# Cross attention, experts and bit-linear layers in one program: where the experts' rows are put back, the order of the second queries, and the place of the output weights' products

## The reference

```python
x = x + L0_xattn(_layernorm(x), ctx)   # 16 heads of 16, plus a second attention on the last 16 context rows
x = x + L0_ffn(_layernorm(x))          # experts, below
x = x + L1_xattn(_layernorm(x), ctx)   # below
x = x + L1_ffn(_layernorm(x))          # bit-linear layers

def L0_ffn(x):                         # E = 16 experts, K = 2 of them for a token, CAP = 128 slots each
    xt = x.reshape(-1, D)                                  # 896 tokens, D = 256
    scores = jnp.sqrt(jax.nn.softplus(xt @ gate_w.T))
    _, idx = jax.lax.top_k(scores + gate_b, K)
    w = scores of the two, divided by their sum
    pos = ...                                              # place of the pair in its expert's slots
    valid = pos < CAP
    buf = zeros((E, CAP, D)).at[e, posc].add(x_pairs)      # rows without a place are dropped
    out = (jax.nn.silu(buf @ W1.T) * (buf @ W3.T)) @ W2.T  # 176 wide
    y_pairs = out[e, posc] * (w.reshape(-1) * valid)[:, None]
    return y_pairs.reshape(T, K, D).sum(axis=1) + (jax.nn.silu(xt @ Ws1.T) * (xt @ Ws3.T)) @ Ws2.T

def L1_xattn(x, ctx):                  # H = 16 heads of 128
    q = rmsnorm((x @ Wq).reshape(B, Sq, H, D), gq)
    k = rmsnorm((ctx @ Wk).reshape(B, Skv, H, D), gk)
    v = (ctx @ Wv).reshape(B, Skv, H, D)
    attn = softmax(einsum('bqhd,bkhd->bhqk', q, k) * D ** -0.5)
    return einsum('bhqk,bkhd->bqhd', attn, v).reshape(B, Sq, H * D) @ Wo
```

## Time and profile before

| what | value |
|---|---|
| median of 3 runs (lowest to highest) | 2377.38 us (2376.2 to 2377.73) |
| the profiled execution, and its span | 2380.05 us, 2378.2 us |
| mean granted TensorE clock in it | 0.935 |
| PE busy | 2121.2 us, 89% of the span |
| DVE busy | 1753.7 us, 74% |
| POOL busy | 1240.3 us, 52% |
| ACT busy | 1183.9 us, 50% |
| moved by the DMA engines | 243.79 MB, mean 103 GB/s |

### The profile page before, as it was taken

How to read it: one execution, slowest core, us unless ns; L and a number is a source line. 1 busy time by engine, 2 the same in 40 slices (tenths; PEclk the granted TensorE clock), 3 DMA queues, 4 the chain that set the end, 5 groups by cost and what they waited for, 6 DMA issues and landing times. The chain is left out here.

```text
span 2378.2 us, 46452 instructions
## 1 busy us (share of the span) xinstructions
PE 2121.2 (89%) x16728; PEld 1697.7 (71%) x16728; DVE 1753.7 (74%) x2341; ACT 1183.9 (50%) x2067; POOL 1240.3 (52%) x993
## 2 busy tenths in 40 slices
PE   4899999999999479999998792978999999999865
PEld 2688788788788357777777541656999999998633
DVE  5788887888888556666674434769999999998367
ACT  1688888888888225565554121542333333333202
POOL 1566666666665133344331113306999999997100
PEclk8999999999999669999999776989999999999977
DMA  2324324324322313334330432342222222220400
GB/s 86 90 93 157 121 92 157 121 94 155 121 106 119 138 67 130 114 121 146 129 112 30 184 93 71 112 135 95 84 80 85 84 102 75 88 93 22 182 0 16
DMA packets 97713, 243.79 MB, mean 103 GB/s; under 512 B 31313, under 2 KB 69106, under 8 KB 88290
## 3 DMA queue, kind: packets, MB, share of 16 engines
q1 hardware_dynamic: 91442, 228.87, 27.3%
q10 hardware_dynamic: 4608, 9.44, 1.0%
...
...
## 5 line engine op out<-in xcount | busy, mean ns | idle before, releaser
L347 DVE TENSOR_REDUCE rk<-n_sq 128x1024 f32 (+2 forms) x384 | 465.8, 1213 | 123.1 <-ACT n_sq L295 120.7
L295 ACT ACTIVATE n_sq<-n_slot 128x1024 f32<-128x1024 f32 (+1 forms) x384 | 394.7, 1028 | 142.7 <-PE n_slot L255 133.2
L253 PE MATMUL n_slot<-n_wh,n_yh 128*128 128x512 f32 (+1 forms) x768 | 318.1, 414 | 9.4 <-PEq L444 9.4
L1704 DVE TENSOR_REDUCE a_mpart<-a_pre 112x2 f32<-112x1024 f32 (+1 forms) x192 | 218.8, 1184 | 118.7 <-PE a_pre L1542 118.7
L255 PE MATMUL n_slot<-n_wh,n_yl 128*128 128x512 f32 (+1 forms) x768 | 302.9, 394 | 0.0
L254 PE MATMUL n_slot<-n_wl,n_yh 128*128 128x512 f32 (+1 forms) x768 | 302.3, 394 | 0.0
L1640 ACT ACTIVATE a_pr<-a_sc 128x448 f32<-128x448 f32 (+1 forms) x384 | 205.4, 545 | 191.1 <-PE a_sc L1571 178.7
L1348 POOL TENSOR_TENSOR p_S<-p_S,a_mb 128x896 f32<-128x896 f32 x94 | 256.4, 2763 | 20.8 <-ACT a_mb L1387 20.8
L227 POOL TENSOR_TENSOR n_khat<-n_kb,n_rs 128x240 f32<-128x240 f32 x192 | 114.6, 597 | 234.3 <-DVE n_rs L362 234.3
L1348 POOL TENSOR_TENSOR a_S<-a_S,a_mb 128x896 f32<-128x896 f32 x84 | 228.8, 2760 | 3.6 <-ACT a_mb L1387 3.6
L1400 ACT ACTIVATE p_S<-p_S 128x896 f32<-128x896 f32 x96 | 91.6, 954 | 171.2 <-POOL p_S L1348 166.8
...
## 6 DMA issues: line engine op xcount, KB each, us to landing
...
```

The source lines that it names most:

```text
L253: pe.matmul(dst, high, wh[:, cols], start=True, stop=False)
L295: act.activation(sq[0:n, w, :], slot[w][0:n, :], ACT.Square).then_inc(slot_free, 1)
L347: dve.tensor_reduce(g.rk[0:n, b, j, 8 * s:8 * s + 8], sq[0:n, (2 * j + s) % 3, :].rearrange("p (h d) -> p h d", h=8), X, ALU.add)\
L1704: dve.tensor_reduce(mpart[:, chunk, k:k + 2], pre[group % 2][0:QP, :, 0:hi - lo], X, ALU.max).then_inc(pre_max, 1)
```

## The change

There are three parts.

*Experts' results are scattered.* A token's row in `xbuf` becomes 257 wide, and the last column holds the number of the pair. ACT copies the rows for the first choice into a new tile `rows` and POOL those for the second and the pair numbers. `xbuf` is filled with empty rows, and a new DRAM buffer `ypairs` with zeros, by two transfers from DRAM to DRAM at the start of `phase_keys`; the zero stores in the MoE go. In the expert loop DVE copies the pair column of each expert's slots to `slot_pair`, and POOL scatters the 128 rows of `ye` to `ypairs` by these numbers, one indirect DMA for each expert; empty slots go to rows behind the used ones. ACT's stores and POOL's 16 gathers go. SP then loads `ypairs` in four transfers, and DVE's 16 additions are as before. The index list `gu` and its three operations go. The loads of the first two parts of Wq and the split of the first one move from the layer norm into the MoE: on SP behind the loads of the experts' weights, on POOL between the two kinds of scatters. The MoE now stands inside the second of the program's two cleanup groups, and some of its buffers lie in tiles of the later attention.

*The order in the queries.* The distances TR, HL and BACK are one less each. In each step ACT does high, root, square, result instead of square, root, high, result, and DVE normalise, low, sums instead of sums, normalise, low.

*The output weights' products.* SP loads Wv and Wo right behind the first tiles of the second batch. PE multiplies in step 0, two pairs behind the scores of each of the tiles 8 to 11, into the banks of the outputs, and ACT copies them there. ACT also scales the second half of the tiles 2, 4, 6, 8 and 10 of step 0, eight activations each. DVE no longer waits for the stored queries ahead of its first scaling but ahead of the first maximum, and adds the five halves that ACT has scaled to the count `s_scaled` at the end of its step 0.

```diff
+            sp.dma_start(g.xbuf[0:E * CAP, :], g.a["empty"]).then_inc(g.empty_out, 16)
+            sp.dma_start(g.ypairs[0:2 * T, :], g.a["zeros"]).then_inc(g.empty_out, 16)
...
-    TR, HL, BACK = 3, 4, NT + 4
+    TR, HL, BACK = 2, 3, NT + 3
...
             for u in range(UNITS + BACK):
+                if 0 <= u - HL < UNITS:
+                    high(u - HL)
+                if 0 <= u - 1 < UNITS:
+                    root(u - 1)
                 if u < UNITS:
                     square(u)
-                if 0 <= u - 1 < UNITS:
-                    root(u - 1)
-                if 0 <= u - HL < UNITS:
-                    high(u - HL)
...
             for u in range(UNITS + BACK):
-                if u < UNITS:
-                    sums(u)
                 if 0 <= u - 1 < UNITS:
                     normalise(u - 1)
                 if 0 <= u - HL < UNITS:
                     low(u - HL)
+                if u < UNITS:
+                    sums(u)
...
             load_next(1, 1)
+            sp.dma_start(g.wv[:, :, :], g.a["L1_WvT"].rearrange("h d c -> d h c")).then_inc(g.wv_in, 16)
+            sp.dma_start(g.M[:, :, :], g.a["L1_Wo"].rearrange("h d n -> d h n")).then_inc(g.wo_in, 16)
             load_next(2, 0)
-            sp.dma_start(g.M[:, :, :], g.a["L1_Wo"].rearrange("h d n -> d h n")).then_inc(g.wo_in, 16)
...
-            sp.dma_start(g.wv[:, :, :], g.a["L1_WvT"].rearrange("h d c -> d h c")).then_inc(g.wv_in, 16)
...
                         for k in range(2):
-                            mm = pe.matmul(ring[m % 2][:, k * D:(k + 1) * D], g.wv[:, 2 * m + k, :], g.M[:, 2 * m + k, :],
+                            mm = pe.matmul(ob[m % 3][:, k * D:(k + 1) * D], g.wv[:, 2 * m + k, :], g.M[:, 2 * m + k, :],
...
                 for j in range(NK):
                     if front:
                         scores(j)
+                    if first and j in WEIGHTS:
+                        weights(*WEIGHTS[j])
...
-                    if last and j == 2:
-                        weights(0, 3)
                     if back and j == 2:
                         spread()
-                    if last and j == LAG:
-                        weights(3, NM)
...
-            for i in range(2):
-                dve.wait_ge(g.q_stored[i], 8 * NG)
...
-                        for half in range(2):
+                        for half in range(1 if first and j in ACT_HALF else 2):
...
                     if front and j == 1:
+                        if first:
+                            for k in range(2):
+                                dve.wait_ge(g.q_stored[k], 8 * NG)
...
+                if first:
+                    dve.sem_inc(s_scaled, len(ACT_HALF))
...
+                def scaled(j):
+                    n, r = rows(j), (2 * j + 1 + (2 if j >= 3 else 0)) % RING
+                    act.wait_ge(s_ready, 2 * j + 2)
+                    for h in range(8):
+                        act.activation(S[i][0:n, j, HALF + h * NQ:HALF + (h + 1) * NQ], ring[r][0:n, h * NQ:(h + 1) * NQ],
+                                       ACT.Copy, scale=g.rk[0:n, b, j, 8 + h:9 + h]).then_inc(act_scaled, 1)
...
+                if isinstance(b, int) and b == 0:
+                    for j in range(NK):
+                        if j in ACT_HALF:
+                            scaled(j)
+                        if j in WEIGHTS:
+                            weights(*WEIGHTS[j])
                 if last:
                     act.wait_ge(q_split, B)
-                    weights(0, 3)
...
-            sp.wait_ge(zeroed, 1)
-            for n in range(0, SLOTS, 1024):
-                sp.dma_start(xbuf[n:n + 1024, :].rearrange("(p a) d -> p (a d)", p=P), zero[:, :]).then_inc(zero_out, 16)
             for n in range(2):
                 load_w(*SPLIT[n], w_in[n])
+            for c in range(2):
+                load_wq(sp, g, c)
...
+            for i in range(2):
+                sp.wait_ge(y_stored[i], 16 * (E // 2))
+            by_tile = ypairs[0:2 * T, :].rearrange("(k t p) d -> p k t d", k=2, t=NT)
+            for n in range(2):
+                for k in range(2):
+                    sp.dma_start(yg[:, k, 4 * n:4 * n + 4, :], by_tile[:, k, 4 * n:4 * n + 4, :]).then_inc(gathered[n], 16)
...
+            pool.tensor_copy(rows[:, :, :, D], pair_id[:, :, :]).then_inc(rows_ready, 1)
+            pool.tensor_tensor(rows[:, 1, :, 0:D], g.xn[:, :, :], g.ones[0:TT, 0:1].unsqueeze(1).broadcast_to([TT, NT, D]),
+                               ALU.mult).then_inc(rows_ready, 1)
+            pool.wait_ge(rows_ready, 3)
+            pool.wait_ge(g.empty_out, 32)
+            pool.wait_ge(steps, 28)
             for t in range(NT):
                 for k in range(2):
                     pool.indirect_dma_start(
                         out=xbuf, out_offset=bass.IndirectOffsetOnAxis(ap=su[:, k * NT + t:k * NT + t + 1], axis=0),
-                        in_=g.xn[:, t, :], in_offset=None).then_inc(scattered, 16)
+                        in_=rows[:, k, t, :], in_offset=None).then_inc(scattered, 16)
+            split_wq(pool, g, 0)
+            for e in range(E):
+                pool.wait_ge(pair_ready, e + 1)
+                pool.wait_ge(y_ready, e + 1)
+                pool.indirect_dma_start(
+                    out=ypairs, out_offset=bass.IndirectOffsetOnAxis(ap=slot_pair[:, e:e + 1], axis=0),
+                    in_=ye[e % 2][:, :], in_offset=None).then_inc(y_stored[e % 2], 16)
             for i in range(2):
                 pool.wait_ge(y_stored[i], 16 * (E // 2))
-            for t in range(NT):
-                for k in range(2):
-                    n = k * NT + t
-                    pool.indirect_dma_start(
-                        out=yg[:, n, :], out_offset=None, in_=ybuf,
-                        in_offset=bass.IndirectOffsetOnAxis(ap=gu[:, n:n + 1], axis=0)).then_inc(gathered[t // 4], 16)
...
+            act.activation(rows[:, 0, :, 0:D], g.xn[:, :, :], ACT.Copy).then_inc(rows_ready, 1)
...
-                    act.wait_ge(y_ready, e + 1)
-                    act.dma_start(ybuf[e * CAP:(e + 1) * CAP, :] if isinstance(e, int) else ybuf[bass.ds(e * CAP, CAP), :],
-                                  ye[1 - i][:, :]).then_inc(y_stored[1 - i], 16)
...
+                    dve.wait_ge(x_in[i], 16 * pair + 16)
+                    dve.tensor_copy(slot_pair[:, n:n + 1] if isinstance(n, int) else slot_pair[:, bass.ds(n, 1)],
+                                    xe[i][:, D:D + 1]).then_inc(pair_ready, 1)
...
-                    n = k * NT + t
-                    dve.wait_ge(gathered[t // 4], 16 * NT)
+                    dve.wait_ge(gathered[t // 4], 32)
...
-            with_normed("l1", lambda: phase_moe(nc, g))
         with nc.cleanup_on_exit():
             with ExitStack() as weights:
                 first_context(nc, g, weights)
                 with ExitStack() as context:
                     query_weights(nc, g, context)
-                    with_normed("l2", lambda: phase_queries1(nc, g), weights=True)
+                    with_normed("l1", lambda: phase_moe(nc, g))
+                    with_normed("l2", lambda: phase_queries1(nc, g))
```

111 lines of the change are left out of this document (57 added, 54 removed).

## The result

The changed kernel took 2351.9 us in the median of four runs (2349.6 to 2355.3), the kernel before 2377.4: a ratio of 0.9893, 95% interval 0.9881 to 0.9905. Four more runs beside other kernels gave 2352.7 (2349.0 to 2353.5), ratio 0.9887 (0.9872 to 0.9902). The gain is 25.5 us where 29.0 was forecast (2348.4, within the range of 2338 to 2360).

A forecast was written before the change was run, and what follows sets the result against it. PE was taken to bound the expert loop and POOL to pace the steady attention, with gains adding between them: -0.4 - 11.9 - 3.2 - 7.5 + 1.0 - 7.0 = -29.0, from median 2377.4 to 2348.4 us, range 2338 to 2360.

The forecast's parts named there:

- Places in a row, gains add: Places between the expert loop and the attention's last step follow one another, so their gains add; forecast sum -29.0 us.
- Router, -0.4: In the router three small DVE operations of 0.17 go, one of them overlapped: -0.4 us.
- Fills, 0: Two DRAM-to-DRAM fills in the first keys phase, hidden by idle DMA engines: cost 0; uncovered 14 us.
- Expert loop, 0: ACT's stores go, DVE's copies and POOL's scatters come, all beside a full PE: 0 us.
- End of the MoE, -11.9: One scatter and four plain loads replace the gathers behind the last expert; sums end 11.9 us earlier, bounds 8 to 13.3.
- a sign of being wrong: At the MoE's end, loads of the pair rows that take over 6 us for two would show the forecast wrong.
- Norm, -3.2: Norm ahead of the queries: POOL's weight split moves to the MoE, freeing the normalisations: -3.2 us, between -2.5 and -3.3.
- Queries, -7.5: Queries: pace 2.45 for 2.71 a unit (-5.2), start +1.4, end -3.7; together -7.5 us, bounds -2.3 to -12.5.
- rival A: Queries stay at 2.71 a unit, bound by the round trip, not the order: 2353.6 us; chance .20.
- Start of the attention and step 0, +1.0: Step 0: PE's eight weight products +4, DVE's savings and earlier start -4.8, weights' wait +2; taken as +1.0, bounds -2 to +5.
- Last step, -7.0: Attention's last step without weight products: outputs start at 2198.1 instead of 2205.58; taken as -7.0 us, bounds -3.5 to -9.1.
- rival B: Step 0 is starved of weights and PE falls to the lower clock: +4, 2352.4 us; chance .14.

The follow-up runs named there:

- Experts alone: Changed experts, fills and layer norm, with queries and second attention as in the kernel before: 2365.0 us, 13.3 under the kernel before.
- the one without attention: Changed experts and changed queries, second attention as in the kernel before: 2358.2 us, 20.1 under the kernel before.
- the version without any of them: Changed kernel with Wv and Wo loaded early and ACT's high part of batch 1's queries behind tile 8 in step 0: 2346.0 us, ratio 0.9860.

## Why the prediction was right, and where it was off

- *Places in a row, gains add:* borne out. Experts alone 13.3, queries on top 6.9, attention on top 5.5 must add up to the whole, 25.6, since each is measured on top of the other; the test is that the queries are worth 7.9 alone and 6.9 on top of the experts. The steady part never moved.
- *Router, -0.4:* the profile has -0.5. *Fills, 0:* the norm ahead of the MoE starts at 1326.5 to 1329.2 in the profiles with the fills and at 1327.0 to 1328.6 without, so nothing of them shows.
- *Expert loop, 0:* off by 1.4 in this profile. The step said that all scatters lie beside a full PE. They do, 2.83 apart; but a scatter holds the result's buffer until it has landed, and at the pipeline's end PE's results come 1.4 apart. That wait is worth 0.95, by the experiment with a buffer of its own for the last result; where the rest lies stays open.
- *End of the MoE, -11.9:* 9.8 measured, within its bounds of 8 and 13.3. The first sums start 9.45 after the last copy, where 7.4 was forecast. Mis-sized: 0.8 between the last copy and POOL's start, and 6.2 for the first loads, where I took 4.7; but the second pair was there with no further wait. Loads of over 6 us were named as a sign of being wrong, and they came.
- *Norm, -3.2:* the size was right (3.3), and so was the mechanism: the single normalisations show that POOL's operations hold them up. The place of the remedy was wrong in the main: I gave all of it to POOL's place; the earlier load alone, with POOL back in the norm, gives 2.5 of it. Not in the sum at all: the boundary of the groups, 1.4 less behind the sums and 1.2 more ahead of the first norm.
- *Queries, -7.5:* 9.4 in the profile, 7.9 and 6.9 by medians. The order, not the distance, is what shortened the unit: 2.40, not 2.71, so rival A is out. The pace was forecast at 2.45 and gives 5.9 from the thirteenth unit on, not 5.2. The start cost 0.3 up to there in the changed kernel (28.5 and 28.2 from the first projection), where 1.4 was forecast. The end gained 3.8 in this profile (forecast 3.7), but only 0.9 in the one without attention.
- *Start of the attention and step 0, +1.0:* from the last copy to the first shift 42.6 before, 42.1 and 43.9 after: -0.6 and +1.3. The sum was near, the path to it was incomplete. I had PE wait 2 for the weights; it waited 0.6 and 1.3, because DVE had already lost 4.2 to ACT, whose stream puts batch 1's queries first. With ACT's wait gone PE waits 3.5. Each hides the other, and with the loads moved a third wait stood in their place, which is why only the version without any of them is faster.
- *Last step, -7.0:* 7.5 in one profile, 5.9 in the other, where the clock fell; of the eight profiles with this step five have some 5.9. The outputs start where the prediction put them, 9.5 after the maxima's spread was formed; 19.8 of outputs follow where the clock stays up. That they would run on without a wait of over 1 us was wrong: there is one of 1.9 ahead of them.
- *The sum:* the executions profiled are 30.4 and 27.4 apart, where 29.0 was forecast; the medians 25.5. The step that failed most is "I carry the sum of differences to the median unchanged": the profiled execution of the kernel before lies 2.7 above its median, the first of the changed kernel 2.3 below. The changed kernel's runs are spread over 6 us, those of the kernel before over 1.5 to 6 depending on the session, and single terms were off by 1 to 2 in both directions. That the profiled difference comes so near to 29.0 is in part luck. So is it that the medians, 2351.9 and 2352.7, lie on rival B's 2352.4: the clock did fall in step 0 in the second profile, but PE waited only 1.3 for the weights there, and the fall cost 1.6 of the 4.
